# Layer 2 of a four-layer graph network in a new order, with its scores taken from the far products

## The reference

```python
Xw = X @ Wv + bv
sj = Xw @ aw[:d, 0]
si = Xw @ aw[d:, 0]
e = leaky_relu(sj[:, None, :] + si[:, :, None] + ab[0], negative_slope=0.2)
alpha_matrix = A * jnp.exp(e)
transition = alpha_matrix / (jnp.sum(alpha_matrix, axis=-1, keepdims=True) + 1e-12)
H, Xk = 0, X
for k in range(3):
    H = H + Xk @ Wk[k] + bk[k]
    Xk = jnp.einsum('bij,bjd->bid', transition, Xk)
return relu(H)
...
x = layernorm(x + layer2(x))
```

## Time and profile before

| | |
|---|---|
| median of 3 runs | 724.49 us (721.04 to 725.16) |
| the profiled execution | 719.44 us, its span 717.6 us |
| layer 0, layer 1 | to about 295 us, to about 390 us |
| layer 2, layer 3 | to about 595 us, to the end |
| busy: PE, DVE, ACT, POOL | 662.0, 566.0, 537.8, 374.5 us |
| instructions | 17119 |

### The profile page before, as it was taken

One profiled execution on the slowest core, in us unless ns is written; L12 is line 12 of the kernel. 1 busy time (PEld: TensorE's weight loads), 2 busy tenths in 40 slices (PEclk: granted clock), 3 DMA queues, 4 the chain that ended last, 5 costly groups with the idle time before them and its releaser, 6 DMA issues.

```text
span 717.6 us, 17119 instructions
## 1 busy us (share of the span) xinstructions
PE 662.0 (92%) x5590; PEld 483.3 (67%) x5590; DVE 566.0 (79%) x1743; ACT 537.8 (75%) x1193; POOL 374.5 (52%) x449
## 2 busy tenths in 40 slices
PE   5899999999999998899995999999999998999985
PEld 4577776677777775566664666666666666787874
DVE  4999999998888877688887768677777765677765
ACT  4578877788887777688886677677767766888875
POOL 1435556554565557466665253534444354676763
PEclk9999999999999999999997899999999998999998
DMA  9664437535354424566654244543444533567663
GB/s 275 152 190 81 98 81 199 132 75 132 76 133 86 77 45 83 109 133 135 136 133 83 62 87 89 90 90 75 101 75 85 82 59 60 111 158 165 138 169 119
DMA packets 176636, 80.04 MB, mean 112 GB/s; under 512 B 122402, under 2 KB 174114, under 8 KB 176548
## 3 DMA queue, kind: packets, MB, share of 16 engines
q1 hardware_dynamic: 166512, 70.54, 41.7%
q0 software_dynamic: 8448, 8.39, 8.3%
q10 hardware_dynamic: 1588, 0.01, 0.1%
HBM read 28.59 MB, written 8.39 MB: 52 GB/s over the span
## 4 chain that ended last, share of the span: by engine, by line
PE 41%; DMA 10%; SPq 3%; DVE 3%; issue 2%; ACT 2%; POOL 2%; ACTq 0%; POOLq 0%; DVEq 0%
PE bank L86 12%; PE bank L88 12%; PE bank L87 12%; DMA xT_lo<-x_halves 10%; SPq L1162 3%; POOL x_halves L1148 1%; PE bank L1467 1%; DVE l_pre L1339 1%; PE bank L1573 1%; PE bank L1252 1%; DVE l_st L1062 1%; ACT l_mid_hi L1627 1%; PE bank L1864 1%; PE bank L1264 1%; ACT x_resident L1096 1%
## 5 line engine op out<-in xcount | busy, mean ns | idle before, releaser
L1096 ACT ACTIVATE x_resident<-l_pre,l_nmr,l_rstd 128x256 f32<-128x256 f32 x256 | 137.8, 605 | 13.4 <-POOL l_nmr L1090 12.7
L991 POOL TENSOR_TENSOR hq<-hq 128x512 f32<-128x512 f32 x48 | 69.8, 1455 | 95.4 <-ACT hq L705 93.1
L1148 POOL TENSOR_TENSOR x_halves<-x_resident,x_halves 128x1024 f16<-128x1024 f32 x46 | 98.0, 2131 | 28.4 <-DVE l_pre L1339 24.3
L86 PE MATMUL bank<-Wk_lo,xT_hi 128*128 128x2 f16 (+2 forms) x384 | 94.4, 275 | 3.2 <-DMA xT_lo<-x_halves 3.2
L87 PE MATMUL bank<-Wk_hi,xT_lo 128*128 128x2 f16 (+2 forms) x384 | 95.3, 274 | 0.0
L88 PE MATMUL bank<-Wk_hi,xT_hi 128*128 128x2 f16 (+2 forms) x384 | 95.0, 273 | 0.0
L1062 DVE BATCH_NORM_STATS2 l_st<-l_pre 128x6 f32<-128x256 f32 x256 | 93.5, 411 | 0.0
L86 PE MATMUL bank<-W2T_lo,h_hi 128*128 128x257 f16 x256 | 71.0, 277 | 4.8 <-ACT zf L717 4.1
L1789 POOL TENSOR_TENSOR l_T_lo<-l_tf,l_T_hi 128x512 f16<-128x512 f32 x16 | 18.7, 1169 | 104.0 <-ACT l_T_hi L1633 104.0
L1087 POOL TENSOR_TENSOR l_rstd<-l_veps,minus_half 128x4 f32<-128x4 f32 x64 | 64.7, 1010 | 12.6 <-DVE l_veps L1076 9.0
L88 PE MATMUL bank<-W2T_hi,h_hi 128*128 128x257 f16 x256 | 71.0, 277 | 0.0
(11 more groups left out here) (206 smaller groups left out, 2019.6 us busy)
## 6 DMA issues: line engine op xcount, KB each, us to landing
adj<-in_adj SPq DMA_DIRECT2D x32, 256.0 KB, 4.0
x_halves<-in_x SPq DMA_DIRECT2D x16, 512.0 KB, 4.2
x_resident<-b_half SPq DMA_DIRECT2D x8, 1024.0 KB, 7.5
x_resident<-in_x POOLq DMA_DIRECT2D x16, 512.0 KB, 6.1
out<-x_resident SPq DMA_DIRECT2D x15, 512.0 KB, 3.2
l_adjT<-adjT_resident SPq DMA_DIRECT2D x16, 256.0 KB, 2.5
x_resident<-in_L_gnn_W SPq DMA_DIRECT2D x2, 512.0 KB, 5.4
x_resident<-in_L_gnn_Wk SPq DMA_DIRECT2D x1, 768.0 KB, 8.6
```

Of the source, the lines that this page charges most:

```text
L86: nc.tensor.matmul(out, lhs[0], rhs[1], start=start, stop=False, **kw)
L991: pool.tensor_tensor(hq[:, 0, :], hq[:, 0, :], hq[:, h, :], ALU.add).then_inc(hqs_ok, 1)
L1096: act.activation(K.x[:, gcols(g, j)], L.pre[p][:, j, :], ACT.Identity, bias=L.nmr[p][:, j:j + 1], scale=L.rstd[p][:, j:j + 1]).then_inc(L. ...
L1148: pool.tensor_tensor(F.xs[p][1], x_group(K, g), F.xs[p][0], ALU.subtract).then_inc(F.x_lo, 1)
```

## The change

In layer 2:

- `project_far` multiplies 258 columns instead of 256, so the scores come out as the last two columns of the far product; `node_scores`, `split_scores` and bank 2 as their place are gone. The halves of the far product hold the scores too (`far0`, `far1`, now one pair of tiles per group, two groups deep), `spread` reads its column from them, and `scores` adds the two halves of the other (`l_si`).
- All four far products of a group run one step ahead, in three banks (2, 0, 1, and 2 again).
- bk is no longer a product. `bk` is loaded to all 128 rows and summed by GpSimd at the start (`K.bk`), and VectorE adds it (`add_bk`); the rectifier is a maximum in `residual`. ScalarE's `relu` and its setup passes are gone.
- `logits` uses the leaky function on ScalarE; VectorE's `leaky` is gone.
- The order of calls in `step` is new on all engines, and `norm_apply` runs a step later.
- The `SEAMS` tables of the borders 1 to 2 and 2 to 3 are new.

In layer 0, `incidence` and `edge_weights` read the bank instead of the copy in SBUF.

The core of the diff:

```diff
-            dve.tensor_scalar(inc[p][:], K.at[:, acols(g)], 0.0, None, ALU.not_equal).then_inc(inc_ok, 1)
+            dve.tensor_scalar(inc[p][:], b_adj[:], 0.0, None, ALU.not_equal).then_inc(inc_ok, 1)
...
-            first = K.at[:, acols(g)].rearrange("p (g n) -> p g n", g=GP)[:, :, 0]
+            first = b_adj[:].rearrange("p (g n) -> p g n", g=GP)[:, :, 0]
...
-    b_s, b_t, b_far, b_near = bank[0], bank[1], bank[2:4], bank[4:8]
+    b_t, b_near = bank[1], bank[4:8]
+    b_far = [bank[0], bank[2], bank[3], bank[0]]
...
-            if j >= 2 or reused(g, 1):
-                pe.wait_ge(far_lo, upto(g, GP, j - 1))
+            if j == 3:
+                pe.wait_ge(far_lo, upto(g, GP, 1))
+            elif reused(g, 1):
+                pe.wait_ge(far_lo, upto(g - 1, GP, (4, 2, 3)[j]))
...
-            pe.matmul(o, K.ones16[:], K.bkrow[:], start=False, stop=False, skip_group_check=True)
...
+        def spread(g, p):
+            pe.wait_ge(far_lo, upto(g, GP, GP))
...
-            act.activation(S.t[:, j * N:(j + 1) * N], b_t[:, j * N:(j + 1) * N], ACT.Identity,
+            act.activation(S.t[:, j * N:(j + 1) * N], b_t[:, j * N:(j + 1) * N], ACT.Prelu, alpha=0.2,
...
-            dve.tensor_tensor(L.pre[p][:, j, :], hr[:, j, :], K.x[:, gcols(g, j)],
-                              ALU.add).then_inc(L.pre_ok, 1)
+            dve.scalar_tensor_tensor(L.pre[p][:, j, :], hr[:, j, :], 0.0, K.x[:, gcols(g, j)], ALU.max,
+                                     ALU.add).then_inc(L.pre_ok, 1)
...
+            dve.scalar_tensor_tensor(hr[:, j, :], b_near[j][:, D:2 * D], 1.0 / WK_SCALE, K.bk[:], ALU.mult,
+                                     ALU.add).then_inc(hr_ok, 1)
...
+            dve.tensor_tensor(si[:], far[p][0][:, :, D + 1], far[p][1][:, :, D + 1], ALU.add).then_inc(si_ok, 1)
...
-            if halves_due(F, g + 1):
-                x_low(K, F, pool, g + 1, q)
-            if has(0):
-                T_low(g, p)
-            if has(-1):
-                norm_scales(K, L, pool, g - 1, q)
+            if halves_due(F, g + 2):
+                x_low(K, F, pool, g + 2, p)
+            if has(1):
+                T_low(g + 1, q)
+            if has(0):
+                norm_scales(K, L, pool, g, p)
```

More of the change, by code:

```diff
@@ L250, in constants @@
         pool.memset(K.minus_half[:], -0.5).then_inc(const, 1)
-        pool.wait_ge(const, 8)
+        pool.wait_ge(const, 7)
     def sum_rows(pool):
[L254 to L257, removed]
+        pool.wait_ge(rows_in, 16)
+        pool.tensor_tensor(K.bk[:], bkn[:, 0, :], bkn[:, 1, :], ALU.add).then_inc(bk_part, 1)
+        pool.wait_ge(bk_part, 1)
+        pool.tensor_tensor(K.bk[:], K.bk[:], bkn[:, 2, :], ALU.add).then_inc(bk_ok, 1)
     def low_w3(pool):
@@ L1491, in layer2 @@
     ts, tT = halves("T", [128, C]), [halves(f"TT{p}", [128, GP, N]) for p in range(2)]
-    far, mid = ([halves(f"{name}{j}", [128, D]) for j in range(GP)] for name in ("far", "mid"))
+    mid = [halves(f"mid{j}", [128, D]) for j in range(GP)]
+    far = [halves(f"far{p}", [128, GP, D + 2]) for p in range(2)]
+    si = sb("si", [128, GP])
     hr = sb("hr", [128, GP, D])
@@ L1565, in walk_far @@
             pe.wait_ge(far_lo, upto(g, GP, j + 1))
[L1566 removed]
+            triple(nc, b_near[j][:, 0:D], [s[:, j, :] for s in tT[p]], [s[:, j, 0:D] for s in far[p]],
                    start=False, skip_group_check=True).then_inc(mid_ps, 1)
@@ L1572, in walk_mid @@
             o = b_near[j][:, D:2 * D]
-            pe.matmul(o, K.ones16[:], K.bkrow[:], start=False, stop=False, skip_group_check=True)
             triple(nc, o, [s[:, j, :] for s in tT[p]], [s[:] for s in mid[j]],
                    start=False, skip_group_check=True).then_inc(out_ps, 1)
+        def spread(g, p):
+            pe.wait_ge(far_lo, upto(g, GP, GP))
+            if reused(g, 1):
+                pe.wait_ge(S.t_ok, upto(g - 1, GP, GP))
+            for j in range(GP):
+                for s in (1, 0):
+                    m = pe.matmul(b_t[:, j * N:(j + 1) * N], far[p][s][:, j, D:D + 1].to_broadcast([128, 128]),
+                                  K.ident16[:], start=s == 1, stop=s == 0)
+            m.then_inc(S.sj_ps, 1)
         def step(g, p, has):
@@ L1748, in step @@
             q = 1 - p
-            if has(1):
-                scores(g + 1)
             if has(-1):
-                residual(g - 1, q, 3)
-                norm_row(L, dve, g - 1, q, 2)
-            if has(0):
-                far_low(g, 0)
-                far_low(g, 1)
-            if has(-1):
-                norm_row(L, dve, g - 1, q, 3)
                 norm_variance(L, dve, g - 1, q, EPS)
             if has(1):
-                leaky(g + 1)
+                far_low(g + 1, q, 2)
+                far_low(g + 1, q, 3)
             if has(0):
-                far_low(g, 2)
-                far_low(g, 3)
+                mid_low(g, 0)
+            if has(1):
+                scores(g + 1, q)
+            if has(0):
+                mid_low(g, 1)
+                mid_low(g, 2)
+                add_bk(g, 0)
+                mid_low(g, 3)
+                add_bk(g, 1)
+                add_bk(g, 2)
             if has(1):
                 transition(g + 1, q)
-            if has(0):
-                mid_low(g, 0)
-                mid_low(g, 1)
-                mid_low(g, 2)
-                mid_low(g, 3)
-            if has(1):
                 row_sums(g + 1)
+                normalised(g + 1)
             if has(0):
@@ L1776, in step @@
                 residual(g, p, 1)
+                norm_row(L, dve, g, p, 0)
+                add_bk(g, 3)
+                norm_row(L, dve, g, p, 1)
                 residual(g, p, 2)
-                norm_row(L, dve, g, p, 0)
-                norm_row(L, dve, g, p, 1)
-            if has(1):
-                normalised(g + 1)
-        return step, 1, 1
+            if has(2):
+                far_low(g + 2, p, 0)
+                far_low(g + 2, p, 1)
+            if has(0):
+                residual(g, p, 3)
+                norm_row(L, dve, g, p, 2)
+                norm_row(L, dve, g, p, 3)
+        return step, 2, 1
     def gpsimd(pool):
```

192 lines of the change are left out of this document (82 added, 110 removed).

## The result

The changed kernel takes **734.98 us** (median of 4 runs, 733.48 to 735.65), the kernel before 724.35 (4 runs, 721.04 to 725.16): **ratio 1.017, 95% interval 1.012 to 1.022**. It is slower by 11 us, where 710.5 was forecast. The profiled run took 735.65 us, its span is 733.6. Runs at a lower granted clock are left out of every ratio and of the medians of the changed kernels, where the only one is a run of old_seams with 843.63 us at a mean granted clock of 0.748 (0.982 to 0.987 in its other runs).

A forecast was written before the change was run, and what follows sets the result against it. PE was taken to bound layer 2, its step falling from 12.26 to 11.3 us. 13.4 (14 steps) - 1.0 - 1.3 (seams) + 3.0 (layer 0) = 14.1 us off the 724.49 median gave 710.5 us, range 703 to 721.

The forecast's parts named there:

- the placing of the bias on VectorE: Layer 2 step: `si` at 1.28 us and bias at 1.48 after PE's first far walk, `mid low 1` at 1.60.
- late transfers: Layer 2: transfers landing late add 0.26 us to each of 14 steps, 3.6 us in all, in the kernel before.
- The slow rival: Layer 2: GpSimd's low half of x catches `si`, 2.1 us more per step, 740 us in all; chance 0.11.
- PE's sum of 10.87: Layer 2: PE's work per step after score products and bk products go; a 0.40 us wait makes the step 11.27.
- the wait before the fourth mid walk: Layer 2: PE waits 0.4 us per step for VectorE's `l_mid_lo`, which stands behind the first `add_bk`.
- VectorE as a bound: Layer 2 rival: if VectorE's passes could not overlap, its 10.7 us become 12.3, step as now, 724 us; chance 0.07.
- Seams: Borders of layer 2: a loss of 1.0 us from layer 1 to 2 and 1.3 from layer 2 to 3.
- Layer 0: Layer 0: reading from PSUM frees VectorE's passes from GpSimd's; 2.7 us back plus 0.3 more, 3.0 gained.
- elsewhere: Layer 0: 0.3 us of gain expected outside the window from 91 to 142 us, on top of 2.7.

The follow-up runs named there:

- old_seams: bias_psum with the five seam tables of the kernel before; 705.7 us (three runs), ratio 0.975 to the kernel before.
- wait_bias: The changed kernel, but GpSimd starts the low half of x only when the next group's bias is written; 707.62 us, ratio 0.980 to the kernel before.
- bias_psum: The changed kernel with the bias read column by column from the far banks in PSUM and `l_si` gone; 705.06 us, ratio 0.9765 to the kernel before.
- low_first: bias_psum with the fourth mid low half ahead of the first `add_bk` on VectorE; 701.42 us, ratio 0.970 to the kernel before.
- after2: The changed kernel run once more, unaltered; 733.77 us, ratio 1.018 to the kernel before.

## Why the prediction was wrong, point by point

**The step that failed is the placing of the bias on VectorE.** The text put `si` at 1.28 us and the bias at 1.48 after PE's first far walk, and GpSimd's low half of x at about 1.44. Counted from the far walk at 488.06 us of the changed kernel's trace, the rows above say 1.29, 1.49 and 1.40. All three places were right to 0.04 us. What was wrong is that only `si`, with its two inputs, was taken as something GpSimd can catch. The bias, 0.04 us behind the start of GpSimd's pass by the forecast's own times, was given 0.12 us of VectorE's time (1.48 to 1.60) without a row for such a pass beside GpSimd. It took 2.05, the step 13.15 instead of 11.3, and the 14 steps 189.6 us where 14 x 11.3 and 3.6 of late transfers make 161.8. It read PSUM before; the change made it read SBUF.

**The chance was wrong too.** The slow rival had this very mechanism, for `si` alone, and said 2.1 us per step and 740; it was given 0.11 because `si` would come 0.15 too early. Two tiny passes in a row, 0.2 apart, against a GpSimd pass of 2.1 us at about the same moment: by these numbers that one of the two is caught is the likely case, and a margin of 0.15 is no reason against it. The measured price is 1.8 us in 13 steps, and 1.7 in each of the four steps with a stretch of half clock, for which the forecast had no term.

**A row of the kernel before showed it.** "GpSimd's tiny passes hold nobody" is true and beside the point. Layer 3 of the kernel before has a four-column pass that is held by the same large pass in ten of the 16 groups (a held and a free one, then GpSimd):

```profile
610.36 0.53 DVE L1069 TENSOR_TENSOR l_mdiff<-l_st 128x4 f32<-128x4 f32 x1
617.90 0.16 DVE L1069 TENSOR_TENSOR l_mdiff<-l_st 128x4 f32<-128x4 f32 x1
```

```profile
608.74 2.13 POOL L1148 TENSOR_TENSOR x_halves<-x_resident,x_halves 128x1024 f16<-128x1024 f32 x1
```

0.53 instead of 0.16, ending at 610.89 with GpSimd's pass at 610.87. With `wcol_hi`, which is a tensor_scalar of four columns just as the bias is, the trace had both held forms. The forecast used for layer 0 and for `si`, and not for the bias that it moved to SBUF in layer 2.

**The rest of the sum, with the hold gone** (wait_bias, bias_psum, low_first):
- PE's sum of 10.87 and the step of 11.3: the undisturbed step is 11.33 in wait_bias and bias_psum; 11.02 without the wait before the fourth mid walk, which was put at 0.4 and is 0.3. Right.
- VectorE as a bound: not at 11.33, as PE's 11.02 with the same passes in another order shows. Right. VectorE was put at 10.7 us and is busy 10.20 in low_first; ScalarE was put at 7.5 and is busy 8.08, which bounds nothing.
- Late transfers: 0.09 us per step in bias_psum (11.42 in the mean), 0.36 in wait_bias; 0.26 was carried over from before. Near enough.
- Seams: layer 2 without its 14 steps is 38.2 us before and 39.8 in bias_psum, a loss of 1.6 against 2.3 forecast. PE's wait before layer 3's first spread is 3.35 in the changed kernel, where 3.5 was given. Right in kind.
- Layer 0: about 2 instead of 3.0. In the window from 91 to 142 us PE gained 2.0 us (49.93 busy against 47.92) where 2.7 was expected, and all of layer 0 is 2.0 shorter: the term was over-sized by the 0.3 "elsewhere" and by taking PE's whole idle time as gone.
- Layer 1 (about 1 us longer) and layer 3 (0.3 to 2 us shorter) move though the change leaves their steps alone; why stays open.
- Together: 705 to 708 without the hold, against 710.5. That it comes so near is in part luck: the seams cost 0.7 less than forecast and layer 0 gave 1.0 less.

## What to carry to other kernels

When an edit moves a small VectorE pass from PSUM to SBUF operands, or adds one, list what GpSimd runs at that moment: where such a pass had started here (1.15 to 2.13 us long), a tensor_scalar between SBUF operands or a pass with two SBUF inputs lasted until it ended, though it had four columns, and everything in VectorE's queue stood behind it. Take the operand from PSUM, use a form that isn't held, or let GpSimd wait for the tiny pass: the runs with each of the three gave 24 to 30 us here. Of that, some 5 to 7 us are TensorE's clock (three stretches at half clock in the 14 steps of after2, four in the first trace): look at the granted clock of single steps before the whole loss is put down to the wait. A margin of a tenth or two between two engines' starts is no argument; if a hold would cost more than the gain, make the order certain by a wait.

## What the runs showed of the hardware that was not expected

- A tensor_scalar over 4 columns with SBUF operands takes 0.23 us alone and 2.05 when it begins 0.09 us into a GpSimd pass of 2.12; behind a pass of 1.15 it takes 1.08. A tensor_reduce of the same 4 columns takes 0.16 in the same place.
- Passes of 256 columns with one operand in PSUM run beside GpSimd at their full pace (0.33 from start to start), and so does a tensor_scalar of 512 columns out of PSUM (0.675; from SBUF it took about 1.2 at the same place).
- With a PE wait of 1.8 us in nearly every step, the granted clock fell to 0.5 for 3.4 us in three or four of the 14 steps, at 1.6 to 1.7 us each; without these waits it did not fall there.
- TensorE's rise to its upper level came at 11 to 13 us or at about 20 us in executions with the same code up to there; the mark after 38 us moved by up to 3.7 us (39.9 to 43.6).
